# Attention with eight PSUM banks: a ring of four score banks that also takes the short uses, and the maxima turned by one transpose

## What is computed

```python
x = x + attn_a(layernorm(x), w_qkv, w_proj)      # causal; scores clipped to +-100, floor of 1e-8
x = x + ffn(layernorm(x), Wq, ..., W1, W2, ...)   # full attention, then one of 4 experts per row
x = x + attn_b(layernorm(x), ...)
x = x + ffn(layernorm(x), Wq, ..., W1, W2, ...)
# in attn_a and ffn, 16 heads of 16 dims, T = 512:
scores = q @ k.T * 16 ** -0.5
p = exp(scores - max(scores, axis=-1)); p = p / sum(p)
out = (p @ v) @ Wo
```

## Time and profile before

| | us |
|---|---|
| median of 3 runs (lowest, highest) | 2593.06 (2582.32, 2595.44) |
| profiled execution | 2579.53 |
| its span, first to last instruction | 2577.8 |
| TensorE busy / VectorE / ScalarE / GpSimd | 2418.6 / 1831.9 / 1438.2 / 1351.5 |
| row maxima on VectorE (L783) | 885.6 |
| exponentials on ScalarE (L704) | 774.7 |
| causal pass of the first call, about | 74 to 626 |
| full passes, about | 626 to 1112 and 1786 to 2275 |

### The profile page before, as it was taken

How to read it: one execution, slowest core, us unless ns; L and a number is a source line. 1 busy time by engine, 2 the same in 40 slices (tenths; PEclk the granted TensorE clock), 3 DMA queues, 4 the chain that set the end, 5 groups by cost and what they waited for, 6 DMA issues and landing times. The chain is left out here.

```text
span 2577.8 us, 45874 instructions
## 1 busy us (share of the span) xinstructions
PE 2418.6 (94%) x14724; PEld 1393.9 (54%) x14724; DVE 1831.9 (71%) x3685; ACT 1438.2 (56%) x2991; POOL 1351.5 (52%) x1358
## 2 busy tenths in 40 slices
PE   6999999999999999989999699988999999989998
PEld 3455555554444444349899366653344434349997
DVE  5999999999778888854333558867778888845333
ACT  3666666666777777753333232214777777653332
POOL 5356666563234554444655579843334454435655
PEclk8999999999999999999999799988999999999999
DMA  5333333333434444324665200015434444335654
GB/s 161 101 105 107 105 102 108 112 105 96 120 112 124 133 129 125 98 93 161 213 201 179 72 1 17 17 58 138 118 109 129 129 130 122 85 118 176 202 194 141
DMA packets 249936, 305.88 MB, mean 119 GB/s; under 512 B 28034, under 2 KB 224865, under 8 KB 249700
## 3 DMA queue, kind: packets, MB, share of 16 engines
q1 hardware_dynamic: 238164, 275.37, 35.8%
q0 software_dynamic: 10176, 26.27, 2.9%
q10 hardware_dynamic: 1360, 1.31, 0.2%
HBM read 210.32 MB, written 92.84 MB: 118 GB/s over the span
## 5 line engine op out<-in xcount | busy, mean ns | idle before, releaser
L783 DVE TENSOR_REDUCE neg_max_af<-sc_af 128x1 f32<-128x512 f32 (+3 forms) x864 | 551.0, 664 | 105.2 <-PE sc_af L489 101.2
L704 ACT ACTIVATE prob_af<-sct_af 128x512 f32<-128x512 f32 (+1 forms) x864 | 484.1, 582 | 234.9 <-PE sct_af L512 231.3
L783 DVE TENSOR_REDUCE neg_max_f<-sc_f 128x1 f32<-128x512 f32 x512 | 334.6, 685 | 93.0 <-PE sc_f L489 90.8
L704 ACT ACTIVATE prob_f<-sct_f 128x512 f32<-128x512 f32 x512 | 290.6, 598 | 127.5 <-PE sct_f L512 126.1
L512 PE MATMUL sct_af<-stack_q_af,stack_k_af 99*128 99x512 bf16 (+3 forms) x1024 | 320.1, 343 | 7.9 <-ACT prob_af L704 7.1
L489 PE MATMUL sc_af<-stack_k_af,stack_q_af 96*128 96x512 bf16 (+3 forms) x1024 | 320.0, 342 | 4.1 <-DVE neg_max_af L783 4.0
L1620 PE MATMUL y_ps_e<-w_r,hT_e 128*128 x1120 | 255.4, 381 | 5.7 <-issue 4.0
L812 DVE SCALAR_TENSOR_TENSOR prob_af<-prob_af,w_r 128x512 f32<-128x512 f32 (+2 forms) x224 | 233.2, 1049 | 21.7 <-ACT prob_af L704 21.5
L1807 DVE TENSOR_TENSOR y_e<-y_ps_e,b_e 128x256 f32<-128x256 f32 x70 | 29.7, 425 | 298.3 <-PE y_ps_e L1620 296.5
L540 PE MATMUL out_af<-prob_af,v_aug_af 128*32 128x512 f32 (+3 forms) x2048 | 231.9, 525 | 8.7 <-DVE prob_af L812 7.8
L1620 PEld LDWEIGHTS y_ps_e<-w_r,hT_e 128*128 128x128 f32 x1120 | 207.2, 190 | 35.3 <-issue 9.4
(11 more groups left out here) (383 smaller groups left out, 4650.0 us busy)
## 6 DMA issues: line engine op xcount, KB each, us to landing
w_r<-in_f_W_dram SPq DMA_DIRECT2D x66, 1024.0 KB, 5.1
stack_k_af<-k_parts_d SPq DMA_DIRECT2D x64, 384.0 KB, 4.3
k_parts_d<-parts_af SPq DMA_DIRECT2D x187, 128.0 KB
q_parts_d<-parts_af SPq DMA_DIRECT2D x96, 128.0 KB
stack_q_af<-q_parts_d SPq DMA_DIRECT2D x64, 192.0 KB, 2.9
stack_k_f<-k_parts_d SPq DMA_DIRECT2D x32, 384.0 KB, 4.2
w_next<-in_f_W_dram SPq DMA_DIRECT2D x12, 1024.0 KB, 4.9
k_parts_d<-parts_f SPq DMA_DIRECT2D x91, 128.0 KB
```

Source lines behind the costliest of these rows:

```text
L704: nc.scalar.activation(dst, src.rearrange("p (h q) -> p h q", h=len(heads)), ACT.Exp).then_inc(S.exp_done, 1)
L783: nc.vector.tensor_reduce(M.neg_max[:, qt, heads[0]:heads[-1] + 1], src, AX.X, ALU.max, negate=True).then_inc(S.max_done, 1)
```

## The change

The two `gen` banks become one, and the ring of score banks gets a fourth. Heavy uses keep the `gen` bank. Light uses take a place in the ring, in the order in which TensorE makes them: every score and every light use is the next place, and the use four places back must have been read (for a score its row maximum, for a light use its reader). In the opening and the closing the uses go to the ring and to `gen` by turns.

The parts of the maxima are laid out as [part, head, tile] in place of [tile, part, head], so that one transpose gives 48 rows of 128 columns in place of four that give 12 rows each. The reader's copy and the DMA's source change shape with it.

```diff
-    bank_of, used_before = {}, {}
-    newest = [None, None]
-
-    def place(use, bank):
-        bank_of[use], used_before[use] = bank, newest[bank]
-        newest[bank] = use
-
-    for at, use in enumerate(opening):
-        place(use, (at + 1) % 2)
+    ring, gen_uses = [], []
+    place_of = {}
+
+    def place(use, uses):
+        place_of[use] = (uses, len(uses))
+        uses.append(use)
+
+    def place_scores(n, g, kt, i):
+        if exists(n) and score_heads(n, kt, i):
+            place(("score", n, g, kt, i), ring)
+
+    def bank(use):
+        uses, at = place_of[use]
+        return M.sc[at % len(M.sc)] if uses is ring else M.gen
+
+    def used_before(use):
+        uses, at = place_of[use]
+        back = len(M.sc) if uses is ring else 1
+        return uses[at - back] if at >= back else None
+
+    for at, use in enumerate(opening[0:8]):
+        place(use, (ring, gen_uses)[at % 2])
+    for g in (0, 1):
+        for kt in range(KT):
+            for i in range(4):
+                place_scores(first, g, kt, i)
+            if 4 * g + kt < 7:
+                place(opening[8 + 4 * g + kt], (ring, gen_uses)[kt % 2])
     for n in range(first, end):
         for s in range(SLOTS_N):
-            if light_at(n, s):
-                place(light_at(n, s), 1)
-            if heavy_at(n, s) and s % 2 == 0:
-                place(heavy_at(n, s), 0)
+            g, kt = divmod(s, KT)
+            light, heavy = light_at(n, s), heavy_at(n, s)
+            for i in range(4):
+                place_scores(*group(n, g + 2), kt, i)
+                if light and i == (2 if kt == KT - 1 else 0):
+                    place(light, ring)
+            if heavy and s % 2 == 0:
+                place(heavy, gen_uses)
...
-                if used_before[use]:
-                    what, m, j = used_before[use]
+                old = used_before(use)
+                if old and old[0] == "score":
+                    pe.wait_ge(S.max_done, max_unit(*old[1:]) + 1)
+                elif old:
+                    what, m, j = old
                     per, sem = READ_OUT[what]
                     pe.wait_ge(sem, per * read_count(what, m) + j + 1)
...
-                    Gb = M.gen_bf[bank_of[use]]
-                    for t in range(KT):
-                        last = nc.tensor.transpose(Gb[0:12, t * P:t * P + P], M.max_parts[:, t, :, :].rearrange("p a h -> p (a h)"), C.ident_bf[:, :])
+                    last = nc.tensor.transpose(bank(use)[:, :].bitcast(BF16)[0:12 * KT, 0:P], M.max_parts[:, :, :, :].rearrange("p a h t -> p (a h t)"),
+                                               C.ident_bf[:, :])
...
-                u = max_unit(n, g, qt, i)
-                if u >= 3:
-                    pe.wait_ge(S.max_done, u - 2)
-                bank = M.sc[u % 3]
+                use = ("score", n, g, qt, i)
+                bank_free(use)
+                ps = bank(use)
...
-                    nc.scalar.activation(M.max_sb[:, j % 2, :], M.gen_bf[bank_of[use]][0:12, 0:T], ACT.Copy).then_inc(S.max_sb, 1)
+                    nc.scalar.activation(M.max_sb[:, j % 2, :], bank(use)[:, :].bitcast(BF16)[0:12 * KT, 0:P], ACT.Copy).then_inc(S.max_sb, 1)
...
-                nc.vector.tensor_copy(M.max_parts[:, :, 0, :], M.neg_max[:, :, :]).then_inc(S.max_split, 1)
+                parts = [M.max_parts[:, p, :, :].rearrange("p h t -> p t h") for p in range(3)]
+                nc.vector.tensor_copy(parts[0], M.neg_max[:, :, :]).then_inc(S.max_split, 1)
...
-    M.max_parts = sb("max_parts", [P, KT, 3, 4], BF16)
-    M.max_sb = sb("max_sb", [12, 2, T], BF16)
+    M.max_parts = sb("max_parts", [P, 3, 4, KT], BF16)
+    M.max_sb = sb("max_sb", [12 * KT, 2, P], BF16)
...
-    M.sc = [psum("sc0"), psum("sc1"), psum("sc2")]
-    M.sct = [psum("sct0"), psum("sct1")]
+    M.sc = [psum(f"sc{i}") for i in range(4)]
+    M.sct = [psum(f"sct{i}") for i in range(2)]
     M.out = psum("out")
-    M.gen = gen
-    M.gen_bf = [t[:, :].bitcast(BF16) for t in gen]
+    M.gen = psum("gen")
```

More of the change, by code:

```diff
@@ L407, in use_bank @@
                 what, n, j = use
-                G = M.gen[bank_of[use]]
+                G = bank(use)
                 if 0 in halves:
@@ L488, in score @@
                     o = at * cols
-                    last = nc.tensor.matmul(bank[:, o:o + cols], M.stack_q[0:96, g, h, qt * P:qt * P + P], M.stack_k[0:96, g, h, 0:cols],
+                    last = nc.tensor.matmul(ps[:, o:o + cols], M.stack_q[0:96, g, h, qt * P:qt * P + P], M.stack_k[0:96, g, h, 0:cols],
                                             start=not masked, stop=True, skip_group_check=masked)
@@ L781, in row_max @@
                 cols = P * (qt + 1) if causal(n) else T
-                src = M.sc[u % 3][:, 0:len(heads) * cols].rearrange("p (h k) -> p h k", h=len(heads))
+                src = bank(("score", n, g, qt, i))[:, 0:len(heads) * cols].rearrange("p (h k) -> p h k", h=len(heads))
                 nc.vector.tensor_reduce(M.neg_max[:, qt, heads[0]:heads[-1] + 1], src, AX.X, ALU.max, negate=True).then_inc(S.max_done, 1)
@@ L828, in add_y @@
                 dst = M.tmp if ffn(n) else M.x_out[n % 2]
-                nc.vector.tensor_tensor(dst[:, 2 * j:2 * j + 2, 0:D], M.gen[bank_of[use]][:, :].rearrange("p (t d) -> p t d", t=2),
+                nc.vector.tensor_tensor(dst[:, 2 * j:2 * j + 2, 0:D], bank(use)[:, :].rearrange("p (t d) -> p t d", t=2),
                                         M.res[:, 2 * j:2 * j + 2, :], ALU.add).then_inc(S.y_sb, 1)
@@ L834, in normalise @@
                     return
-                G = M.gen[bank_of[("out", n, g)]]
+                G = bank(("out", n, g))
                 dve.wait_ge(S.out_ps, NG * n + g + 1)
@@ L1237, in psum @@
         return ctx.enter_context(nc.psum_tensor(f"{name}_{tag}", [P, T], F32))
-    gen = [psum("gen0"), psum("gen1")]
     M = Names()
```

12 lines of the change are left out of this document (6 added, 6 removed).

## The result

The changed kernel takes 2598.7 us (median), beside 2590.3 us of the kernel before in runs taken with it. The ratio is 1.0030, 95% interval 1.0018 to 1.0041: slower by 7.8 us, with 4.7 to 10.6 us as interval (the two medians differ by 8.4). That is within the 0.5% that the prediction called no change, but on the other side of the -3.4 us that it summed. The profiled execution has a span of 2594.5 us, where that of before had 2577.8.

What follows compares the result with a forecast made beforehand. TensorE's stream was taken to bound the full passes, TensorE (groups 1, 2) and VectorE (3, 0) the causal pass. Transposes -11.9, full-pass waits +7.9, causal wait 0, opening +0.6: -3.4 us, median 2589.7, range 2575 to 2604.

Steps and rivals of the forecast that it cites:

- the causal pass, booked at -2.7 us: Causal pass: one transpose saves 0.17 us in groups 1 and 2 of 8 batches, 2.7 us; the ring costs 0.
- Cost 0: Causal group 0: the first score waits 1.1 us for `normalise` in seven batches, hidden by later holds that VectorE already sets.
- VectorE writes the parts of the maxima at a stride: VectorE's strided writes of the maxima, 16 elements an instruction: taken as 0, within a few hundredths of a us.
- The sign that was set for a mis-sized pass: Causal group 0: the pv product moving by over 0.3 us would show the causal pass was mis-sized.
- The bounds of that step: Causal group 0: cost of the new wait between 0 and 7 x 1.1 = 7.7 us.
- The transposes in the full passes: Full passes: one transpose for four saves 0.17 us in 54 of 62 groups, 9.2 us; eight lie ahead of ScalarE's wait.
- rival D: Transposes: 48 columns cost what four times 12 did, no gain, 8.5 us of waits stay; 2602 us, chance 0.10.
- The new waits in the full passes: Full passes: the first score of kt = 3 waits for `normalise`; 1.4 + 8.4 - 1.9 = 7.9 us lost.
- The opening: Opening: group 1's last score waits for ScalarE's second read of a projection, 0.3 us in two calls, 0.6 us.
- Rival B: The wait hides, transposes pay everywhere and the third score's 0.6 us hold goes in eight batches: -21 us, 2572, chance 0.12.
- Rival C: Held scores lose their weight load's cover, 0.10 us in 94 groups, waits at full price: +15.6 us, 2609, chance 0.10.
- All of it is wrong if stages outside attention move: Test of the whole forecast: stages outside attention, which the change doesn't touch, should not move.

Runs made afterwards that it cites:

- e1: Kernel before with only the new maxima layout and one transpose of 48 columns, banks as they were: 2583.9 us, ratio 0.9979.
- e2: Changed kernel with the old maxima layout and four transposes of 12 columns, so the ring alone: 2596.6 us, ratio 1.0046.
- e5: Kernel before with a small VectorE memset ahead of the clip at kt = 0 of each causal group: ratio 1.0022.
- e8: Changed kernel with a GpSimd memset only ahead of the causal split (j = 3) that meets group 1's clips: 2592.0 us, ratio 1.0001.
- e10: e1 plus a GpSimd memset only ahead of the causal split (j = 3) that meets group 1's clips: ratio 0.9962 to the kernel before.
- e3: Changed kernel with `normalise` moved ahead of VectorE's third row maximum: 2601.8 us, ratio 1.0058.
- e4: Changed kernel with a GpSimd memset of 0.31 us ahead of each split of the causal pass: ratio 1.0032.

## Why the prediction was wrong

- **The step that failed: the causal pass, booked at -2.7 us** as "Cost 0" for the ring and -2.7 for the transposes. Measured +5.0, so 7.7 us of the 11.2 us between the forecast and the measured +7.8. The wait was sized rightly (forecast 1.1 us of hold, measured 1.01), and it does cost nothing: kernels with and without the ring have the same batch period (70.33 and 70.36, 70.71 and 70.74), and the transposes gained 3 to 4 us there, for 2.7 booked. What failed is that the lengths of VectorE's instructions were taken as given. The prediction followed VectorE, TensorE and ScalarE behind the wait and never GpSimd, whose subtraction started within 0.02 us of the clip in five of seven batches of the trace of before. So the pair of clips could take 3.1 or 4.3 us, and a shift of 0.02 us could choose. The term that the prediction had at nothing, "VectorE writes the parts of the maxima at a stride [...] I take 0, between a few hundredths of a us more and less", was right in size, and those 0.02 us are what tipped the pair in e1; in e2 the ring did it by making GpSimd early, in e5 a memset. e8 undid it.
- **The sign that was set for a mis-sized pass,** a pv product later by over 0.3 us, came up (281.65 for 281.12, 0.53), but not for the reason it was set for: all of it was there before the held score, from the long clips of earlier batches.
- **The bounds of that step.** 0 to 7.7 us was worked out from the wait, and the loss is of that size by another mechanism: luck. The predicted sum would have come to +4.3 at the upper bound, which a range of 2575 to 2604 holds, as it holds the 2598.7.
- **The transposes in the full passes.** Booked -9.2 us, 0.17 a group. Measured -3.2 and -4.1, -7.3 in all. The unit is right: line 472 starts at 909.62 and the next matmul at 909.79, 0.17 us, where 0.32 stood. The count was not: in e1's last pass TensorE waits 14 times for ScalarE's probabilities, 6.7 us, where before it waited 7 times, 4.4 us. More groups than the booked four a pass lie ahead of a wait that ScalarE ends; the 2.3 us of added wait are what 31 groups at 0.17, 5.3 us, lack to the 3.2 measured (2.1). 48 columns cost no more than 12 did, against rival D.
- **The new waits in the full passes.** Booked 9.8 us at full price and 7.9 with half of the late ones absorbed. Measured by e2: +5.3 and +4.1, 9.4 us (8.8 with the later profiles as base), of which up to 1.7 us in the last pass can be the clock's. The list of places was right (935.32 starts 0.06 behind the end of `normalise`, as booked); whether the half that was to be absorbed was absorbed, these numbers can't tell. At full price, 9.8, and with the transposes at 7.3, the full passes come to +2.5, where +2.1 was measured (+1.7 and 495.5, 496.7 and 496.4 against 495.8).
- **The opening** was 0.6 us; the first `normalise` starts at 88.8 against 88.6 and 87.3. No more can be said.
- **Rival B** had two things right in the causal pass, that the wait hides and that the transposes pay there, and missed the pair of clips as the forecast did. The 0.6 us a batch that it hoped for from the third score didn't come: e2's batches are no shorter than e5's. **Rival C**, lost cover of a weight load, asked for a start over 0.1 us behind the releaser: 279.78 + 0.41 = 280.19 to 280.25 is 0.06, and 934.84 + 0.42 = 935.26 to 935.32 is 0.06. It is out, though the load does lose its lead (it starts at 935.32 with its matmul). **Rival D**'s 2602 lies next to the measured 2599, but its ground is false: the transposes did gain, and its sum has no loss in the causal pass. Its waits in the full passes are there.
- **"All of it is wrong if stages outside attention move"** was a bad test: they move by over 4 us between two profiles of one kernel.
- What stays open: why the clock falls in one batch and not in the next. The causal pass of one profile each shows 3.2 and 3.4 us. Over whole programs the record has more: the mean granted clock is 0.973 over the 20 executions of the changed kernel, and 0.976 over each of four other sets of the kernel before (17 to 35 executions), and over e1's and e2's twelve. So the changed kernel does run at a somewhat lower clock at large, and how much of the +7.8 us goes with that is not shown.

## What to carry to other kernels

When a change moves an engine's queue by half a microsecond, look for the pairs of VectorE and GpSimd instructions that start close together in the trace of before, not only for the waits on the path: which of the two is first was worth a microsecond each time here, and shifts of 0.02 to 0.07 us flipped it in six kernels. Judge the parts of a change in the stage that repeats from profile to profile (here the last full pass, to 0.4 us) and not by the span. If a change gains in its own part and loses by such a pair, an instruction of a third of a microsecond on the engine that has time can put them back in order: e8 shows it for the changed kernel (1.0030 to 1.0001), and e10 keeps the transposes and leaves the ring (0.9962).

## What the runs showed of the hardware

- A clip of 128x1024 on VectorE, two SBUF inputs, took 1.2 us alone and 2.1 to 2.2 us with a subtraction of 128x512 under way on GpSimd; that one took 1.16 us when it was first and 2.25 when it was not. In the rows of the profile GpSimd counts as first from a lead of 0.04 us on, and not with 0.02. Row maxima of 128x512, which read PSUM, stayed at 0.68 beside GpSimd.
- Three comparisons of 128x21 took 5.27, 0.22 and 2.18 us in place of 0.23 each beside GpSimd's instructions of 128x1024 (e3). They seem to stand until one of these is done: the first ends at 2307.39 and the third at 2309.63, some 0.05 us behind the ends of two products (2305.15 + 2.19 and 2307.42 + 2.17), and the second fits in the gap. The first stood through two of them. That reading is argued, not tested.
- The clock fell to half for 6 us behind 1.2 us of idle TensorE (e4), and at the start of the local attention, three windows of 10 us from 1480 us on were granted 0.56, 0.50 and 0.58 in the changed kernel and 0.94, 1.00 and 1.00 in e10, in code that is the same. A batch of e4 with the first took 72.35 us where one without took 69.70, 2.6 us more; the second goes with 4 us of difference between two profiles of one kernel.
